# Post-norm transformer block on one core: the last but one sequence's feed-forward output cut in pieces, and the attention's rows normalised by ScalarE

## The reference

```python
q = rotary((x @ Wq + bq).reshape(B, T, 16, 32).transpose(0, 2, 1, 3))   # 16 heads
k = rotary((x @ Wk + bk)[:, None]); v = (x @ Wv + bv)[:, None]          # one key and value head
attn = softmax(q @ k.T / sqrt(32)); ctx = attn @ v
x = layernorm(x + ctx @ Wo + bo)
w1, w2, w3 = (clip(round(w / (mean(abs(w)) + 1e-8)), -1, 1) for w in (w1, w2, w3))
x = layernorm(x + (sigmoid(x @ w1.T) * (x @ w2.T)) @ w3.T)              # 1408 hidden columns
```

## Time and profile before

| | |
|---|---|
| Runs | median 656.75 us of 3 (656.2 to 657.54) |
| Profiled execution | 652.95 us, its span 651.1 us |
| Mean granted TensorE clock | 0.946 of 2.4 GHz |
| Busy over the span | PE 86%, DVE 75%, ACT 62%, POOL 43% |

### The profile page before, as it was taken

How to read it: one execution, slowest core, us unless ns; L and a number is a source line. 1 busy time by engine, 2 the same in 40 slices (tenths; PEclk the granted TensorE clock), 3 DMA queues, 4 the chain that set the end, 5 groups by cost and what they waited for, 6 DMA issues and landing times.

```text
span 651.1 us, 9112 instructions
## 1 busy us (share of the span) xinstructions
PE 559.8 (86%) x2964; PEld 277.5 (43%) x2964; DVE 486.5 (75%) x675; ACT 403.0 (62%) x825; POOL 280.3 (43%) x370
## 2 busy tenths in 40 slices
PE   6678968969689999989589999987799989969984
PEld 2454544434344444444344444443444434424431
DVE  1867777668889897889999879879798968254332
ACT  1697797565676887756688877566688846013300
POOL 1319789786436314766344425663472200020001
PEclk9889989989889999989899999989699979969998
DMA  7571623048879997999899978879798959200001
GB/s 283 182 279 24 218 69 128 17 103 156 158 168 192 189 184 113 185 157 190 156 193 216 196 137 145 158 179 179 140 218 155 181 105 167 71 0 1 0 1 64
DMA packets 217102, 92.11 MB, mean 141 GB/s; under 512 B 204384, under 2 KB 205536, under 8 KB 216544
## 3 DMA queue, kind: packets, MB, share of 16 engines
q1 hardware_dynamic: 209952, 77.61, 57.4%
q0 software_dynamic: 6144, 12.60, 9.6%
q10 hardware_dynamic: 960, 1.33, 0.6%
HBM read 20.20 MB, written 4.19 MB: 37 GB/s over the span
## 4 chain that ended last, share of the span: by engine, by line
PE 60%; DVE 16%; issue 8%; ACT 6%; DMA 5%; POOL 2%; SPq 1%; DVEq 0%; POOLq 0%; ACTq 0%
PE a_ps L1189 10%; PE b_ps L1201 6%; PE a_ps L1120 6%; PE s_ps L1227 5%; PE b_ps L1189 5%; PE a_ps L1201 4%; DVE p_all L935 4%; PE e_ps L1189 4%; DMA pt_sb<-p_all 4%; PE c_ps L1279 3%; PE b_ps L1174 3%; DVE sh_sb L928 2%; PE c_ps L1265 2%; PE s_ps L1174 2%; PE e_ps L1120 2%
## 5 line engine op out<-in xcount | busy, mean ns | idle before, releaser
L665 ACT ACTIVATE p_all<-s_ps,sh_sb 128x512 f32<-128x512 f32 x192 | 130.2, 683 | 104.7 <-DVE sh_sb L928 101.2
L928 DVE TENSOR_REDUCE sh_sb<-s_ps 128x2 f32<-128x1024 f32 x96 | 116.8, 1217 | 41.2 <-PE s_ps L1227 41.2
L935 DVE SCALAR_TENSOR_TENSOR p_all<-p_all 128x1024 f16<-128x1024 f32 x96 | 128.3, 1336 | 3.1 <-ACT p_all L673 2.9
L673 ACT ACTIVATE p_all<-p_all 128x1024 f16<-128x1024 f32 x96 | 101.7, 1059 | 2.0
L1189 PE MATMUL a_ps<-late,q 128*128 128x512 f16 x352 | 85.2, 386 | 5.2 <-ACT th L636 3.6
L1227 PE MATMUL s_ps<-k_st,q_st 128*128 128x512 f32 x192 | 82.9, 517 | 7.1 <-ACT p_all L665 4.0
L512 POOL TENSOR_SCALAR rstd<-mv 128x1 f32<-128x1 f32 x32 | 10.7, 334 | 166.4 <-DVE mv L893 166.3
L397 POOL DMA_DIRECT2D q_st<-hi x96 | 49.6, 519 | 70.5 <-PE s_ps L1227 34.7
L1120 PE MATMUL a_ps<-xT_sb,wq_sb 128*128 128x512 f32 x104 | 57.0, 682 | 6.2 <-DMA wq_sb<-in_wq 6.2
L1189 PEld LDWEIGHTS a_ps<-late,q 128*128 128x128 fp8e4 x352 | 32.1, 99 | 49.5 <-issue 9.3
L490 POOL TENSOR_TENSOR rot<-raw,table_sb 128x512 f32<-128x512 f32 x20 | 26.1, 1303 | 61.8 <-ACT raw L607 58.3
(11 more groups left out here) (128 smaller groups left out, 948.6 us busy)
## 6 DMA issues: line engine op xcount, KB each, us to landing
q_st<-hi POOLq DMA_DIRECT2D x96, 64.0 KB, 3.1
q_st<-lo POOLq DMA_DIRECT2D x96, 64.0 KB, 3.6
late<-in_w SPq DMA_DIRECT2D x2, 2816.0 KB, 11.1
xT_sb<-in_xT SPq DMA_DIRECT2D x8, 512.0 KB, 5.3
late<-in_x SPq DMA_DIRECT2D x4, 1024.0 KB, 7.0
out<-late SPq DMA_DIRECT2D x16, 256.0 KB, 3.3
late<-in_w SPq DMA_DIRECT2D x2, 1408.0 KB, 7.0
q_st<-hi SPq DMA_DIRECT2D x32, 64.0 KB, 2.0
```

The source lines that it names most:

```text
L665: act.activation(p_pair[n][:, t % 2, :], pair_banks(h * PAIRS + t // 2)[:, t % 2, :], ACT.Exp, bias=sh_sb[:, 2 * n + t % 2:2 * n + t % 2 + ...
L673: act.activation(p_half[n][:, 0, :], p_pair[n].rearrange("p t k -> p (t k)"), ACT.Copy, scale=P_SCALE).then_inc(p_hi, 1)
L928: dve.tensor_reduce(sh_sb[:, 2 * n:2 * n + 2], pair_banks(h * PAIRS + i), AX.X, ALU.min).then_inc(maxed, 2)
L935: dve.scalar_tensor_tensor(out=p_half[n][:, 1, :], in0=p_pair[n].rearrange("p t k -> p (t k)"), scalar=P_SCALE, in1=p_half[n][:, 0, :], op ...
```

## The change

Three things change.

1. In the last head stage (b = 3) `sums2` moves from k=29 to k=25. `dn0` of sequence 2 is cut into three pieces by hidden tiles (`da0`, `db0`, `dc0`: 0 to 3, 4 to 7, 8 to 10) at k=26, 27 and 28, and the output projection of the last sequence's row tiles 0 and 1 is begun at k=25, 30 and 31 (`wa`, two head groups; `wb`, the third) in banks `a` and `e`. `dn1`, `dn2` and `dn3` of sequence 2 move behind the heads: `dn1` in two pieces before and after the last context, `dn2` and `dn3` around the first two row transposes. Each score bank gets its own pair of semaphores.
2. The norm of the attention's rows moves from VectorE to ScalarE in all sequences (`h_rows`): an ACTIVATE Identity with scale 1/std and a bias of minus mean times 1/std, both a column per tile. GpSimd computes that bias (`shift`) behind the power. The last sequence's rows go to the memory of the softmax pairs (`h_last`), as `h_sb` is still in use.
3. At the very end the eleventh hidden tile of `dn0` and `dn1` comes after the ten others of both, and VectorE's tail is reordered.

```diff
-LAST_BESIDE = {25: [], 27: [], 30: []}
-TAIL = ([("dn3", B - 2), ("sums3", B - 1)] + [(f"ht{t}", B - 1) for t in range(TT)]
+LAST_BESIDE = {25: [("sums2", 0), ("wa0", 0)], 26: [("da0", -1)], 27: [("db0", -1)], 28: [("dc0", -1)],
+               29: [("ctx2", 0)], 30: [("wa1", 0)], 31: [("wb0", 0), ("wb1", 0)]}
+TAIL = ([("dn0", B - 2)] + [(f"wo{t}", B - 1) for t in range(TT)] + [("sums3", B - 1)]
+        + [(f"dn{t}", B - 2) for t in range(1, TT)] + [(f"ht{t}", B - 1) for t in range(TT)]
...
@@ banks_of @@
+    if kind == "wo" and s == B - 1:
+        return [("a", "e", "s0", "s1")[n]]
+    if kind == "dn" and s == B - 2:
+        return [("b", "s3", "s2", "s3")[n]]
+    if kind == "dn" and s == B - 1:
+        return [f"s{n}"]
-        return [("eabe" if s == B - 1 else "abae")[n]]
+        return [("abeb" if s == B - 1 else "abae")[n]]
...
@@ SP, at k = 12 @@
-                        sp.wait_ge(normed, norm_count(b - 1, 0, TT - 1))
+                        sp.wait_ge(h_ready, b * TT)
...
@@ GpSimd, inverse_std @@
+                if ln == 0:
+                    pool.wait_ge(rstd_done, n)
+                    pool.tensor_scalar(shift[:, t:t + 1], mv[:, ln, t, 0:1], rstd[:, ln, t:t + 1], -1.0, ALU.mult,
+                                       ALU.mult).then_inc(shift_done, 1)
...
@@ ScalarE @@
+            def h_rows(s, t):
+                act.wait_ge(shift_done, s * TT + t + 1)
+                if s < B - 1:
+                    act.wait_ge(h_free[t], (s + 1) * 16)
+                else:
+                    act.wait_ge(turned[0], (B - 1) * H * PAIRS // PSLOTS * 16)
+                    act.wait_ge(turned[1], (B - 1) * H * PAIRS // PSLOTS * 16)
+                act.activation(h_of(s)[:, t, :], xb[:, t, :], ACT.Identity, bias=shift[:, t:t + 1],
+                               scale=rstd[:, 0, t:t + 1]).then_inc(h_ready, 1)
...
+                    if k in (6, 7, 9, 10):
+                        h_rows(s, (6, 7, 9, 10).index(k))
-                    if k in (13, 20, 29):
-                        norm_row(b, (13, 20, 29).index(k))
+                    if k in (13, 20, 26 if b == B - 1 else 29):
+                        norm_row(b, {13: 0, 20: 1}.get(k, 2))
...
             for t in range(TT):
-                h_high(B - 1, t)
+                h_rows(B - 1, t)
+                if t:
+                    h_high(B - 1, t - 1)
+            h_high(B - 1, TT - 1)
...
@@ VectorE, heads @@
-                    if k in (7, 8):
-                        norm(s, 0, k - 7)
...
                     if k == 10:
-                        norm(s, 0, 2)
                         h_low(s, 0)
-                        norm(s, 0, 3)
                         h_low(s, 1)
...
@@ VectorE, behind the heads @@
+            ffn_out(B - 2, 0)
             normalise(B - 1, HG - 1)
+            norm(B - 2, 0)
+            ffn_out(B - 2, 1)
+            attended(B - 1, 0)
+            attended(B - 1, 1)
+            norm(B - 2, 1)
+            attended(B - 1, 2)
+            h_low(B - 1, 0)
+            attended(B - 1, 3)
+            h_low(B - 1, 1)
+            h_low(B - 1, 2)
+            h_low(B - 1, 3)
             for f in range(FT):
                 gate(B - 1, f)
+                if f in (0, 1):
+                    ffn_out(B - 2, 2 + f)
+                if f in (1, 2):
+                    norm(B - 2, 1 + f)
                 g_low(B - 1, f)
...
@@ TensorE, behind the heads @@
+            pe.wait_ge(expd, B * H * TT - 2)
+            project_out(B - 1, 2, range(HG - 1))
+            project_out(B - 1, 3, range(HG - 1))
+            pe.wait_ge(expd, B * H * TT)
+            down(B - 2, 1, range(0, 7))
             turn_sums(B - 1, HG - 1)
             context(B - 1, HG - 1)
+            down(B - 2, 1, range(7, FT))
             for t in range(TT):
                 project_out(B - 1, t, range(HG - 1, HG))
+            down(B - 2, 2)
+            turn_h(B - 1, 0)
+            turn_h(B - 1, 1)
+            down(B - 2, 3)
+            turn_h(B - 1, 2)
+            turn_h(B - 1, 3)
             for f in range(FT):
                 up(B - 1, f)
+            down(B - 1, 0, range(FT - 1))
+            down(B - 1, 1, range(FT - 1))
+            down(B - 1, 0, range(FT - 1, FT))
+            down(B - 1, 1, range(FT - 1, FT))
+            down(B - 1, 2)
+            down(B - 1, 3)
```

More of the change, by code:

```diff
@@ L139, in banks_of @@
     if use[:4] == "sums":
-        return ["a" if s == 0 else "e"]
+        return ["a" if s == 0 else "s2" if use == "sums3" and s == B - 1 else "e"]
     if use[0] == "q":
@@ L151, in fill_order @@
     fills["e"] += [("kp", 1), ("ks", 1)]
+    fills.update({f"s{n}": [] for n in range(4)})
     for b in range(1, B):
@@ L223, in layer @@
         rstd = sb("rstd", [P, 2, TT])
+        shift = sb("shift", [P, TT])
         nhalf = sb("nhalf", [P, 1])
@@ L327, in layer @@
         rstd_done = sem("rstd_done")
+        shift_done = sem("shift_done")
+        h_ready = sem("h_ready")
         normed = sem("normed")
@@ L1026, in heads @@
                         if b > 1:
-                            norm(r, 1, 3)
+                            norm(r, 3)
                         pairs(b, "q2")
@@ L1055, in heads @@
                         pairs(b + 1, "q0")
[L1056 to L1060, removed]
+                    if b < B - 1:
+                        if k in (27, 29):
+                            ffn_out(s, (k - 27) // 2)
+                        if k == 28:
+                            norm(s, 0)
                             halves(b + 1, "q0")
-                    if b < B - 1:
                         if k == 29:
@@ L1106, in _ @@
                 if t:
-                    norm(B - 1, 1, t - 1)
-            norm(B - 1, 1, TT - 1)
+                    norm(B - 1, t - 1)
+            norm(B - 1, TT - 1)
         @block.tensor
@@ L1168, in project_out @@
             def project_out(s, t, groups=range(HG)):
-                ps, (done, _), _ = out_bank(s, t)
-                if groups[0] == 0 and s < B - 1:
+                ps = wide_bank(f"wo{t}", s)[:, :]
+                if groups[0] == 0:
                     pe.wait_ge(*free(f"wo{t}", s))
@@ L1191, in up, with down @@
                     mm.then_inc(filled(f"up{f}", s, half)[0], 1)
-            def down(s, t):
+            def down(s, t, tiles=range(FT)):
                 ps = wide_bank(f"dn{t}", s)
-                pe.wait_ge(*free(f"dn{t}", s))
-                pe.wait_ge(rounded, 3 * PIECES)
-                for f in range(FT):
-                    if t == 0:
+                if tiles[0] == 0:
+                    pe.wait_ge(*free(f"dn{t}", s))
+                    pe.wait_ge(rounded, 3 * PIECES)
+                for f in tiles:
+                    if t == 0 or s == B - 1:
                         pe.wait_ge(*drained(f"up{f}", s, 1))
@@ L1338, in use @@
                     project_out(s, n)
+                elif kind == "da":
+                    down(s, n, range(0, 4))
+                elif kind == "db":
+                    down(s, n, range(4, 8))
+                elif kind == "dc":
+                    down(s, n, range(8, FT))
+                elif kind == "wa":
+                    project_out(s, n, [0, 1])
+                elif kind == "wb":
+                    project_out(s, n, [2])
                 elif kind == "ht":
```

97 lines of the change are left out of this document (38 added, 59 removed).

## The result

The changed kernel took 637.65 us in the median of 4 runs (633.99 to 641.54), the kernel before 656.48 in 4 beside them (655.99 to 657.54): a ratio of 0.973, 95% interval 0.968 to 0.978. The forecast was 638.2 (635.0 to 643.0). The profiled execution of after took 638.78 us (span 637.0, mean granted clock 0.949 against 0.946); before's took 652.95. So the profiled pair shows 14.2 us and the medians 18.8.

The account below looks back on a forecast made before the run. TensorE was taken as bound by matmuls, so only idle and low-clock time could be won: 11.8 + 1.8 + 2.3 + 2.7 = 18.6 us off 652.95 gives 634.35, plus 3.8 to the runs' median: 638.2 (635.0 to 643.0).

Parts of the forecast that it names:

- From scores 25 to the first up: Last head stage: the same matmuls laid out again start the first up projection at 568.9 instead of 580.71, 11.8 us saved.
- The three waits: TensorE's idle times left in the rearranged end: 0.87 before da0, 1.0 before wb0, 1.5 before the first up projection.
- rival B: Rearranged end waits: last p transposes land 3 us late or the clock falls before up0; 641 to 643 us, chance 0.18.
- First up at full clock and the last downs: After the last heads: up0 at full clock saves 1.8 us; tile 10 coming later and the score banks' end save 2.3.
- 3.08 us of that 11.8: First down projection of tile 0, last head stage: 7.84 us against its twin's 4.76, 3.08 lost at 1.2 GHz.
- The norm: 2.7 forecast: Three head stages: VectorE's queue loses four norms each, two of which count 0.45 us, 0.9 per stage, 2.7 in all.
- rival C: Head stages: shorter waits leave the granted clock up, 1.5 us for each of two stages and more; 635 us, chance 0.13.
- Rival A: Early stages give nothing, as something like a transfer takes the place of VectorE's queue; 640.9 us, chance 0.16.
- the gap of 0.68: ScalarE at k=6, between projection copy and next exponential: the h row, taken as 0.70 us, would be hidden there.
- are read seven and more pairs on: GpSimd's stacks of heads 7 and 8, up to 1 us later behind the shift, are needed only seven pairs on.
- Rival D: ScalarE stands 1.8 us at each of twelve h rows, exponentials behind it; slower than before, 662.5 us, chance 0.02.
- a price of zero for short waits: Rearranged end: remaining waits of 0.9 to 1.5 us leave the clock up, cost zero, with 3.1 as the other end.

Follow-up runs that it names:

- e3: Kernel before with only the last down projections reordered, tile 10 of row tiles 0 and 1 behind their other tiles, banks unchanged: 656.13 us, ratio 1.0013 to before.
- e2: Changed kernel with the norms back on VectorE and no shift on GpSimd, the rearranged end kept: 638.36 us, ratio 0.9747 to the kernel before.
- e5: The changed kernel run again, nothing altered, beside the variants on its chip: 638.47 us, ratio 0.9676 to the kernel before.
- e6: Changed kernel with the last four down projections back in banks b and a, tile 10 still behind the others: 640.54 us, ratio 0.9746 to before.
- e8: Changed kernel with h transpose banks e, b, a, e and the next transposed x load at k=19 instead of 13: 636.51 us, ratio 0.9687 to before.
- e11: Changed kernel with the last down projections in plain order, tile by tile, but still in the score banks: 638.08 us in one run.
- e1: Kernel before with only the norm of the attention's rows on ScalarE and GpSimd's shift, old end: 648.84 us, ratio 0.9895 to before.
- e7: Changed kernel with sums2 and the first output projection pieces moved behind the first down piece: 637.54 us, ratio 0.972 to the kernel before.
- e9: Changed kernel with the x load at k=26 instead of 12 and its bias additions at the next stage's start: 637.28 us, ratio 0.9737 to before.
- e10: Changed kernel with both the late x load and h transpose banks e, b, a, e: 632.0 us, ratio 0.9655 to the kernel before.
- e4: Changed kernel with the head stages' h transposes in banks e, b, a, e instead of a, b, a, e: 636.87 us, ratio 0.9693 to before.

## Why the prediction was right, and where it wasn't

The kinds of loss were the right ones, and the end of the kernel went as laid out. That the total met the measured one within 1 us is in part luck: the profiled pair shows 14.2 us and the medians 18.8, and the sum took one execution's clock as given, which e3 shows to vary (below). I also wrote that a measurement tells 0.2%; it tells half a per cent.

- **From scores 25 to the first up: 11.8 forecast, 11.3 measured**, 50.2 to 50.4 us in after, e2, e5, e6 and e8 alike. Relaying the same matmuls from durations of the trace was accurate to half a microsecond over 50. The three waits were forecast at 0.87, 1.0 and 1.5 and are 0.63, 0.94 and 1.66. The last context's inputs were in time, as counted; rival B had nothing to stand on.
- **First up at full clock and the last downs: 1.8 + 2.3 forecast, 3.9 measured.** The size was right, the mechanism of the second was not. The step that failed is "tile 10 comes after 20 of tile 0's and 20 of tile 1's matmuls, 8.6 us for a wait of 2.1": tile 10's place wins nothing (e3, e6), the wait was for bank b, and the change's move of these sums to the score banks ended it (e11). I had both edits before me and priced only the one whose description fitted. The profile's releaser, VectorE's g_low of tile 10, is the same for both causes: the instruction both fills tile 10 of the gate and empties bank b.
- **3.08 us of that 11.8 were not a fixed price.** (Against 4.92 us, the timeline's figure for a twin, it was 2.92; the first up's 1.8 was 1.6 in the same way, 3.51 against 1.89.) I took the low clock after the 3.04 us wait for its consequence. Three kernels with this same stretch show 7.84, 6.61 and 4.92 us for the 22 matmuls. By which execution of the old end one compares, the piece is worth 11.3 (before), 10.1 (e3) or 7.1 (e1, 57.34 us). Of the last, 1.2 us are no matter of the clock: with the norm on ScalarE e1's last rows come to the first up sooner.
- **The norm: 2.7 forecast; the waits say 0.8 per stage.** 3.58 + 3.66 became 3.21 + 3.21 in all stages of the six kernels with the norm on ScalarE and the old banks and loads (e1, after, e5, e6, e7, e11), and stay in before, e2 and e3: 0.82 against 0.9. The waits were forecast near 3.1 and 3.2. From the first output projection to the first up the traces show more, 1.3, 1.45 and 1.9 us in the three stages (means of three kernels with the norm on VectorE: 40.86, 39.42, 39.91; of the six: 39.54, 37.97, 38.05), 4.6 in all. Part of what lies beyond the waits is rival C's: the first transpose of the third head stage, for one, took 0.63 us in all six, and 1.09, 0.63 and 0.71 in before, e2 and e3. Between the stages the means lose 1.2 us (+1.5 from the second to the third, -0.3 from the first to the second), but there single traces of the six range over 5 us (98.86 to 104.05 from the first to the second), so this loss isn't clear of scatter. Net the traces give about 3.5 us. Rival A had a real wait in mind, and e9 and e10 point to its source, the x load; that it grew with the change isn't shown: the waits of the up projections for ScalarE's tanh average 4.3 us over the three stages in before, e2 and e3 and 4.4 in the six.
- **Open:** e1's ratio makes 6.9 us of the norm alone (4.7 to 9.1 by the interval's ends), where the traces account for 3.5 and 1.2 more in its last rows (12.31 us from the last output projection's start to the first up, before 13.47). The clock may hold the rest: in the median e1's runs have a mean granted clock of 0.945 and the compared runs of before beside them 0.936, while the two profiled executions show 0.950 and 0.946. By my estimate 0.009 of mean clock is 12 us less at 1.2 GHz, worth up to 6 us. Whether the moved norm is what kept the clock up, no trace shows. After against e2 shows 0 to 5. e1's and e2's parts add to 0.964 (0.9895 less 0.0253); after measured 0.973 and 0.968. Within the scatter of several us I can't say whether the norm is worth 3.5 or 6.
- **Prices that I took wrong.** ScalarE's timeline in the third head stage of after:

```profile
447.61 0.67 ACT L626 ACTIVATE raw<-e_ps,small_sb 128x512 f32<-128x512 f32 x1
448.18 0.80 ACT L654 ACTIVATE late<-late,shift,rstd 128x512 f32<-128x512 f32 x1
...
448.96 0.69 ACT L695 ACTIVATE p_all<-s_ps,sh_sb 128x512 f32<-128x512 f32 x1
...
456.28 0.63 ACT L635 ACTIVATE hi<-rot 128x512 fp32r<-128x512 f32 x1 [1.41 <-DMA q_st<-lo]
```

The h row took 0.80 us, not 0.70, and the exponentials start right behind it at 448.96: the gap of 0.68 is used up, and the exponentials don't start late for it. In the Trainium skill, "ScalarE: Activation LUTs", section "What ACT_TABLE_LOAD costs", 186 ns, 0.833 per element and 93 per pointer operand make an estimated 0.80; the trace agrees. The last line is a wait that I had missed: I wrote that the delayed stacks "are read seven and more pairs on", but their source buffer is wanted again before that, and ScalarE's next high half waits 1.41 us for the stack's transfer to end. The wait stands in all three stages of all ten kernels with the norm on ScalarE (1.31 to 1.92 us) and in none of before, e2 and e3. It isn't hidden from ScalarE: the exponentials behind it start at 456.81, 0.6 us after their row maxima end (456.18). What TensorE pays for that, no run separates. A moved transfer has two readers to check: who needs its result, and who needs its source back.

- **Rival D** never came near: no h row released an exponential late. What did hold exponentials is the stack's transfer above, 0.6 us in this row.

## What to carry to other kernels

When a wait's releaser both fills a buffer and empties another, price the edits that lift either; a kernel with only one of them is the cheapest way to tell. Matmuls laid out again from measured durations give an end within half a microsecond; the clock after a long wait does not come with that precision, so keep it as a range of its own. When a wait is lifted, look for the next releaser in the same place: e4's banks took VectorE out of two waits, and TensorE then stood about as long for ScalarE (6.2 us for 6.4 in the first stage). Two edits that bring next to nothing alone may still be worth trying together (e4, e9 and e10), though here the lead over the changed kernel isn't settled.

## What the hardware did that I had not expected

What a wait of some 3 us does to the clock is not fixed. Before and e3 have the same instructions up to their last down projections, and after 3.04 us of idle time in both the same 22 matmuls took 7.84 and 6.61 us: that differs by the execution alone. After 2.93 us in e1 they took 4.92; whether by chance or for the 0.11 us, no run tells. After 2.94 in e7 the first 8 took 3.20 instead of 1.90. Nor does the length of one wait decide. The up projection behind 3.12 us in the first head stage of before took the full-speed 1.90 (the row is under the result), while TensorE's timeline of e6, second head stage, has the half-speed time behind a shorter wait:

```profile
349.50 3.50 PE L1219 MATMUL a_ps<-late,q 128*128 128x512 f16 x8 [2.15 <-ACT th L664]
```

After the same 2.14 or 2.15 us before the last down projections, before, e1, e3 and e6 ran at full speed (20 matmuls in 4.49 us). And from 567.24 to 580.71 of before no wait was longer than 1.50 us, but the first up ran at half speed. So a price of zero for short waits, as I had it, isn't safe either. In the runs of the kernel before that are compared, the time falls as the mean granted clock rises (correlation -0.61 over 38 runs).

A small GpSimd instruction takes five times as long beside VectorE's p_low. GpSimd's and VectorE's timelines of after, two of the twelve shifts of the head stages, the stack's issue behind the second, and VectorE's instructions beside them:

```profile
443.88 0.27 POOL L538 TENSOR_SCALAR shift<-mv,rstd 128x1 f32<-128x1 f32 x1
...
448.85 1.34 POOL L538 TENSOR_SCALAR shift<-mv,rstd 128x1 f32<-128x1 f32 x1
450.14 1.09 POOL L416 DMA_DIRECT2D q_st<-hi  x2
```

```profile
443.92 1.22 DVE L961 TENSOR_REDUCE sh_sb<-s_ps 128x2 f32<-128x1024 f32 x1
...
448.85 1.22 DVE L968 SCALAR_TENSOR_TENSOR p_all<-p_all 128x1024 f16<-128x1024 f32 x1
```

One element per partition cost 0.27 us beside VectorE's reduction from PSUM, and 1.34 when it started together with VectorE's p_low, whose operands are in SBUF; it ended 0.1 us after that. Seven of the twelve took 1.02 to 1.34 us, all beside a p_low. My bounds were 0.22 to 0.56. The Trainium skill, "GPSIMD Engine Reference", section "Specifications", lets the two engines share their way into SBUF and expects contention when VectorE reads two SBUF inputs, as p_low does. The trace agrees; it adds that the small instruction took as long as VectorE's whole one. The h row didn't wait for it: ScalarE came to this one at 451.41, 1.2 us after the shift and not the 2 or more that I had written. But the stack's issue did. It stands behind the shift on GpSimd's queue, so the 1.34 us are what makes the stack late, and with it ScalarE's high half by 1.41 us.
